# Overflow tiles of a mixture of experts: up products in high and low halves, weights loaded in two parts

## The reference, cut to what matters

```python
scores = softmax(t @ gate_w.T)
weights, indices = top_k(scores, 2)
y = zeros_like(t)
for e in range(16):
    w_e = sum(where(indices == e, weights, 0.0), axis=-1)
    y = y + ((silu(t @ w1[e].T) * (t @ w3[e].T)) @ w2[e].T) * w_e[:, None]
z = (silu(t @ sw1.T) * (t @ sw3.T)) @ sw2.T
x = x + tanh(g_ffn[1]) * (y + z)
```

## Time and profile before

| | us |
|---|---|
| median of three executions | 909.65 |
| the profiled execution | 908.75 |
| its span, first to last instruction | 907.0 |
| first up product of an overflow tile starts | 840.63 |
| down product of the last tile starts | 883.00 |
| granted TensorE clock, mean over the span | 0.997 of full speed |

### The profile page before, as it was taken

The page is one execution under the profiler, slowest core; times in us unless marked ns, Lnnn a source line. Parts: engine busy times, 40 slices in busy tenths (PEclk is TensorE's granted clock), DMA queues, the critical chain, the costliest instruction groups (busy, mean ns, idle before and its releaser), DMA issues.

```text
span 907.0 us, 16248 instructions
## 1 busy us (share of the span) xinstructions
PE 885.2 (98%) x6896; PEld 726.0 (80%) x6896; DVE 506.5 (56%) x787; ACT 349.2 (39%) x510; POOL 153.2 (17%) x146
## 2 busy tenths in 40 slices
PE   5999999999999999999999999999999999999997
PEld 5968787878787878788999888887788888877656
DVE  5554454453545455785344344699657387776225
ACT  4633424334333333665253311344652454444110
POOL 0022223132223131210000000014003312222110
PEclk9999999999999999999999999999999999999999
DMA  9011010101020103049900100700221599999837
GB/s 342 20 36 36 1 35 1 35 1 36 1 83 1 36 1 116 1 95 275 303 14 1 44 4 0 285 1 2 109 84 67 206 348 362 358 359 313 294 138 267
DMA packets 30760, 106.87 MB, mean 118 GB/s; under 512 B 3522, under 2 KB 4546, under 8 KB 26978
## 3 DMA queue, kind: packets, MB, share of 16 engines
q1 hardware_dynamic: 25154, 87.46, 27.9%
q0 software_dynamic: 4672, 16.82, 5.8%
q10 hardware_dynamic: 864, 1.57, 0.5%
HBM read 87.18 MB, written 18.66 MB: 117 GB/s over the span
## 4 chain that ended last, share of the span: by engine, by line
PE 87%; DVE 7%; ACT 3%; issue 1%; POOL 0%; DMA 0%; DVEq 0%; ACTq 0%; POOLq 0%
PE ps L645 21%; PE ps L646 19%; PE ps L647 19%; PE ps L1116 6%; PE ps L707 3%; PE ps L1102 3%; PE ps L722 2%; PE ps L923 2%; PE ps L921 2%; PE ps L922 2%; PE ps L755 1%; PE ps L1064 1%; PE ps L1065 1%; PE ps L1066 1%; DVE arena L1828 1%
## 5 line engine op out<-in xcount | busy, mean ns | idle before, releaser
L645 PE MATMUL ps<-arena_r 128*125 128x512 f32 (+2 forms) x544 | 206.8, 380 | 2.9 <-DVE arena_r L1533 2.9
L646 PE MATMUL ps<-arena_r 128*125 128x512 f32 (+2 forms) x544 | 198.9, 366 | 0.0
L647 PE MATMUL ps<-arena_r 128*125 128x512 f32 (+2 forms) x544 | 198.8, 366 | 0.0
L645 PE MATMUL ps<-hT,arena_r 128*128 128x448 f32 (+1 forms) x368 | 136.5, 371 | 0.5 <-DVE hT L1563 0.3
L647 PE MATMUL ps<-hT,arena_r 128*128 128x448 f32 (+1 forms) x368 | 134.5, 366 | 0.0
L646 PE MATMUL ps<-hT,arena_r 128*128 128x448 f32 (+1 forms) x368 | 134.5, 365 | 0.0
L645 PEld LDWEIGHTS ps<-arena_r 128*125 128x125 f32 (+1 forms) x544 | 102.7, 189 | 21.9 <-issue 4.0
L647 PEld LDWEIGHTS ps<-arena_r 128*125 128x125 f32 (+1 forms) x544 | 102.3, 188 | 13.9
L646 PEld LDWEIGHTS ps<-arena_r 128*125 128x125 f32 (+1 forms) x544 | 102.6, 189 | 10.9
L1190 ACT ACTIVATE arena<-arena,mbias,mscale 125x448 f32<-125x448 f32 x96 | 66.1, 752 | 99.5 <-DVE arena L1640 99.5
L2093 POOL TENSOR_TENSOR arena<-arena 125x448 f32<-125x448 f32 x28 | 32.3, 1154 | 259.0 <-ACT arena L1190 259.0
(11 more groups left out here) (252 smaller groups left out, 1328.5 us busy)
## 6 DMA issues: line engine op xcount, KB each, us to landing
land_e<-in_e SPq DMA_DIRECT2D x16, 1408.0 KB, 7.9
arena<-in_e SPq DMA_DIRECT2D x21, 512.0 KB, 7.6
sorted_rows<-arena POOLq DMA_DIRECT2D x1, 7453.0 KB, 60.6
arena<-in_e SPq DMA_DIRECT2D x5, 1408.0 KB, 6.4
land_c<-in_ctx SPq DMA_DIRECT2D x8, 752.0 KB, 4.4
arena<-sorted_rows SPq DMA_DIRECT2D x21, 257.0 KB, 10.1
land_w<-in_gu SPq DMA_DIRECT2D x8, 512.0 KB, 17.9
arena<-in_e SPq DMA_DIRECT2D x21, 192.0 KB, 9.8
```

The costliest lines, as they stand in the source:

```text
L645: mm(into, a[0], w[0], start=begins and i == 0, stop=False)
L646: mm(into, a[0], w[1], start=False, stop=False)
L647: last = mm(into, a[1], w[0], start=False, stop=ends and i == len(operands) - 1)
```

## The change

The up products of the overflow tiles are formed from high and low parts, as those of tiles 0 to 15 are. ACT's `rows_save` is replaced by `rows_high`, and ACT gets `overflow_high`, two copies of 128x1408 per tile. DVE gets `overflow_low`, two subtractions of 128x1408 per tile, and `rows_low`. The order of weights and rows on SP's queue changes: the up weights come as two transfers of 128x1408, half 0 counted on `up_ld[0]` together with the rows, half 1 on `up_ld[1]`; the down weights stay on `dn_ld[0]`. `w_landed` goes up by three per tile instead of two. The wait for half 0 and the rows of the tile before stands at the head of SP's turn, and the next half 0 is issued behind it, before the wait for half 1.

```diff
-            def load_up_of(e, n):
-                sp.dma_start(arena[:, bass.ds(A_E + n % NSLOT * 4352, 2816)],
-                             e13_in[bass.ds(e, 1)].rearrange("o p w -> p (o w)")).then_inc(up_ld[0], 16)
+            def load_up_of(e, n, half):
+                sp.dma_start(land_x[:, bass.ds(n % NSLOT * 4352 + half * 1408, 1408)],
+                             e13_in[bass.ds(e, 1), :, half * 1408:(half + 1) * 1408].rearrange("o p w -> p (o w)")
+                             ).then_inc(up_ld[half], 16)
...
             with sp.Fori(NE + 1, tiles) as n:
                 e = expert_of(n)
+                sp.wait_ge(up_ld[0], n * 32)
+                sp.sem_inc(w_landed, 1)
                 sp.wait_ge(gu_mm, n - 3)
                 sp.wait_ge(row_read, n - 3)
-                load_up_of(e, n)
+                load_up_of(e, n, 0)
+                load_rows_of(n)
+                sp.wait_ge(up_ld[1], n * 16)
+                sp.sem_inc(w_landed, 1)
+                load_up_of(e, n, 1)
                 sp.wait_ge(dn_ld[0], n * 32)
                 sp.sem_inc(w_landed, 1)
                 sp.wait_ge(d_mm, n - 3)
                 load_down_of(e, n)
-                sp.wait_ge(up_ld[0], n * 32 + 32)
-                sp.sem_inc(w_landed, 1)
...
             def up_expert(n):
-                w = A_E + n % NSLOT * 4352
-                pe.wait_ge(w_landed, n * 2 + 1)
-                pe.wait_ge(xg_sv, n + 1)
+                pe.wait_ge(w_low, n * 2 + (nth("sh2") + 2))
+                pe.wait_ge(ln_T, n + (4 * NT + 1))
+                high, low = n % 2 * (28144 - A_E13), A_E - A_E13 + n % NSLOT * 4352
                 for j in range(2):
-                    for k in range(KC):
-                        last = mm(ps[:, 4 + j, 0:EI], xgT[:, k, :],
-                                  arena[:, bass.ds(w + (k * 2 * EI + j * EI), EI)], start=k == 0, stop=k == KC - 1)
+                    last = product(ps[:, 4 + j, 0:EI], [([half[:, k, :] for half in xgT_r],
+                                                         [split_x[:, bass.ds(half + (k * 2 * EI + j * EI), EI)]
+                                                          for half in (high, low)]) for k in range(KC)])
                 last.then_inc(gu_mm, 1)
...
+            def overflow_high(n):
+
+                high, low = n % 2 * (28144 - A_E13), n % NSLOT * 4352
+                for i in range(2):
+                    act.wait_ge(w_landed, n * 3 + (i + 1))
+                    fn(split_x[:, bass.ds(high + i * 1408, 1408)], land_x[:, bass.ds(low + i * 1408, 1408)], ACT.Copy
+                       ).then_inc(w_high, 1)
...
             with act.Fori(NE - 1, last2) as n:
                 silu_tile(n)
-                rows_save(n + 1)
+                rows_high(n + 1)
                 place(n + 2)
+                overflow_high(n + 2)
...
+            def overflow_low(n):
+
+                high, low = n % 2 * (28144 - A_E13), n % NSLOT * 4352
+                for i in range(2):
+                    dve.wait_ge(w_high, n * 2 + (nth("sh2") + i + 1))
+                    v.tensor_tensor(split_x[:, bass.ds(A_E - A_E13 + low + i * 1408, 1408)],
+                                    land_x[:, bass.ds(low + i * 1408, 1408)],
+                                    split_x[:, bass.ds(high + i * 1408, 1408)].bitcast(F32), ALU.subtract
+                                    ).then_inc(w_low, 1)
...
             with dve.Fori(NE + 1, last1) as n:
+                overflow_low(n + 1)
                 tile_hidden(n)
+                rows_low(n + 1)
                 row_ends(n + 1)
                 tile_out(n - 1)
                 tile_hidden_save(n)
```

More of the change, by code:

```diff
@@ L242, in flamingo @@
         land_e = [landing(f"land_e{i}", A_W[i], 2816) for i in range(NSLOT)]
+        land_x = landing("land_x", A_E, (NSLOT - 1) * 4352 + 2816)[1]
         e13 = [halves((4352, 28144)[e % 2], A_W[e % NSLOT], land_e[e % NSLOT], KC, 2 * EI) for e in range(NE)]
@@ L250, in flamingo @@
         smoe = at(10184, EI)
-        xgT = at(47616, KC, P)
-        xgT_r = at_r(47616, KC, P), at_r(31000, KC, P)
+        xgT_r = [nc.alloc_sbuf_tensor_at(name, [P, KC, P], F32R, offset=base + 4 * off)[:]
+                 for name, off in (("xg_high", 47616), ("xg_low", 31000))]
+        A_E13 = 4352
+        split_x = nc.alloc_sbuf_tensor_at("split_x", [P, 28144 + 2816 - A_E13], F32R, offset=base + 4 * A_E13)
         A_XR = 44288
@@ L593, in _ @@
             sp.wait_ge(up_ld[0], 16 * NE)
-            load_up_of(e, NE)
+            load_rows_of(NE)
+            load_up_of(e, NE, 0)
+            sp.wait_ge(up_ld[1], 16 * NE)
+            load_up_of(e, NE, 1)
             sp.wait_ge(d_mm, NE - 4)
@@ L615, in _ @@
                 load_down_of(e, n)
-                sp.wait_ge(up_ld[0], n * 32 + 32)
-                sp.sem_inc(w_landed, 1)
+            sp.wait_ge(up_ld[0], tiles * 32)
+            sp.sem_inc(w_landed, 1)
+            sp.wait_ge(up_ld[1], tiles * 16)
+            sp.sem_inc(w_landed, 1)
             sp.wait_ge(dn_ld[0], tiles * 32)
@@ L1111, in down_expert @@
                 else:
-                    pe.wait_ge(w_landed, n * 2 + 2)
+                    pe.wait_ge(w_landed, n * 3 + 3)
                 if not (isinstance(n, int) and n == 0):
@@ L1459, in _ @@
             last3, last2, last1, tiles = counts(act)
-            def rows_save(n):
-                act.wait_ge(xg_tr, n + 1)
-                fn(xgT, ps[:, 6, :].rearrange("p (k t) -> p k t", k=KC), ACT.Copy).then_inc(xg_sv, 1)
             def silu_tile(n):
@@ L1469, in place @@
             def place(n):
-                act.wait_ge(w_landed, n * 2 + 1)
+                act.wait_ge(w_landed, n * 3 + 1)
                 if not (isinstance(n, int) and n == NE):
@@ L1492, in _ @@
                     expert_high(n + 2)
+            def overflow_high(n):
[4 more added lines that the diff above has]
+                       ).then_inc(w_high, 1)
             act.sem_inc(xs_rdy, NE)
             place(NE)
+            overflow_high(NE)
             with act.Fori(NE - 1, last2) as n:
                 silu_tile(n)
-                rows_save(n + 1)
+                rows_high(n + 1)
                 place(n + 2)
+                overflow_high(n + 2)
             silu_tile(last2)
-            rows_save(last1)
+            rows_high(last1)
             silu_tile(last1)
@@ L2042, in _ @@
                     expert_low(n + 2)
+                else:
+                    overflow_low(n + 2)
             tile_hidden(NE)
+            rows_low(NE + 1)
             row_ends(NE + 1)
```

5 lines of the change are left out of this document (2 added, 3 removed).

## The result

| | before | after |
|---|---|---|
| median, us | 909.48 (20 executions) | 912.34 (20 executions) |
| lowest and highest, us | 907.13, 911.94 | 906.77, 916.12 |
| ratio of the times | | 1.0031, 95% interval 1.0021 to 1.0041 |
| profiled execution, its span | 908.75, 907.0 | 910.41, 908.5 |
| first up product of an overflow tile starts | 840.63 | 839.66 |

The changed kernel is slower by about 0.3%, 2.8 us. That is less than the 0.5% called telling ahead of the prediction, but with twenty executions of each the interval excludes no change. The forecast was 0.3 us less than before.

A forecast was written before the change was run, and what follows sets the result against it. PE, 87% of the chain, was taken as nearly level with the chain of output scatters. Waits ate most of PE's -4.1 us; mostly the early -0.8, plus 0.5 for scatters, gave -0.3 us: 909.3 us, range 906.0 to 912.9.

The forecast's parts named there:

- PE's product: Up products of the five overflow tiles: 3.92 us instead of 4.74 each, -4.1 us on PE if nothing delays it.
- Addresses on PE: Address instructions in the up blocks of tiles 17 to 20: +2.9 us if fully exposed, taken as hidden, 0.
- Rival C: PE's sequencer: addresses are exposed in the overflow up products, +1 to +2.6 us, 911.5; chance 0.06.
- the last up load issued before 858: Sign on SP's queue: tile 20's up load, which went out at 860.23 before, is issued earlier than 858.
- is worth nothing to PE directly: SP's last load ending 3 to 4 us earlier gains PE nothing directly, since no row has PE waiting for a load.
- add half a microsecond for scatters 13 to 15: Output scatters of tiles 13 to 15 share the DMA engines with denser loads: +0.5 us.
- DVE as the pacemaker behind the gap: After tile 16's output copy, tile 19's up product waits for DVE's subtractions and `rows_low`, until 866.6 instead of 865.17.
- "early" case: Loads end earlier, so tile 17's output copy comes at 867.1, not 869.33; tile 20's up product ends 0.8 us earlier.
- Rival A: Scatters of tiles 13 to 15 land in some 5 us each, tile 16's copy never late: -1.5 to -4.7 us; chance 0.15.
- Rival D: Half 1 of tile 20's up weights lands late, so ACT, DVE and `rows_low` end late: +0.9 us; chance 0.05.
- Rival B: DVE's subtractions hold POOL's scatter issue for tile 16, +3.8 us, or tile 17 too, +5.4, 915.0; chance 0.08.
- own range of the forecast: Overflow tiles: -0.8 us to +2.3, the upper end with three scatters at 6.7 us each and tile 17's copy late.

The follow-up runs named there:

- old_loads_again: Second run of the changed kernel with SP's queue as in the kernel before (whole up loads, late wait): 909.37 us, 0.9985 of before.
- one_early: Changed kernel with up weights in one transfer, its wait at the head of SP's turn: 912.93 us, 1.0030 of before.
- late_split: Changed kernel with both waits for the up halves moved to the end of SP's turn: 911.99 us, 1.0030 of before.
- after_again: The changed kernel measured once more, nothing altered: 911.81 us, 1.0022 of before.
- new_loads: Kernel before with plain products and only SP's queue of the change (halves, early waits): 914.72 us, 1.0049 of before.
- halves_late: Kernel before with plain products, up loads in halves, both waits at the end of SP's turn: 910.28 us, 1.0011 of before.

## Why the prediction was off

- **PE's product, -4.1 us: right.** 3.92 to 3.97 us against 4.74, five times. The 3.56 us that the prediction set beside it didn't show, as rows 3 had said.
- **Addresses on PE, 0: right.** L660's address instructions take 46 ns at the median, 125 at most, and the block with them is 0.05 us longer than the one without. Rival C has no part. The trace's answers on two single lines of the changed kernel, L660 and the scatters of L2207 (durations in ns, min/median/max; then from issue to landing):

```profile
L660 PEldq FUSED_REGOPS  x32: 46/46/125, 847.5 to 877.6; - x32
...
L2207 POOL DMA_INDIRECT token_rows<-arena,to_row x5: 976/977/2371, 864.7 to 889.7; - x5
...
DMA to landing us min/median/max: 2.7/4.0/6.1
```


- **SP, "the last up load issued before 858": right**, 853.75 and 856.07. That it "is worth nothing to PE directly" holds for the early loads; the halves are another matter. With whole loads PE waits up to 1.06 us at a time behind the split weights (`old_loads_again`; 1.29 in `one_early`), with late halves 0.37 (`late_split`), which the prediction didn't see. What it does to the scatters is where the sum failed.
- **The step that failed: "add half a microsecond for scatters 13 to 15, which now share the DMA engines with denser loads".** The copy of tile 16 came 3.55 us later, seven times as much, in two parts. The three scatters took 863.18 - 842.81 = 20.37 us, 6.8 each, against 860.60 - 842.15 = 18.45 before: +1.9, about the upper bound that I had worked out (1.7, from 6.7 each) and not the half microsecond that I took. And the first of them went out 842.81 - 839.66 = 3.15 us after the up product of tile 16 began, against 842.15 - 840.63 = 1.52: +1.6, which no term of mine held, because I let the delay begin only at that scatter; the one ahead of it, of tile 12, took 9.0 us against 7.1. The split is that of one execution. In `after_again` the three scatters took 21.35 us, +2.9, and the first of them went out 1.61 us after the up product, as before. Over all runs only the first part holds (20.4 to 22.9 us against 17.8 to 19.3). I took the denser loads for a small correction to a scatter that the trace had shown under light load, and the early end of the loads for the main thing.
- **A term that was missing: the clock.** After 5.29 us without work the down product ran at a granted clock of 0.56 and took 2.05 us longer. The sum priced idle time at its own length.
- **DVE as the pacemaker behind the gap: covered up.** The sum let the up product of tile 19 wait for the subtractions. It didn't: the slow down product ran until 869.47, and `rows_low`, which had begun at 867.82 and took 0.68, was done by then. Where the gap is short the wait is there: in `old_loads_again` PE waits 0.37 us for the hidden product and 0.19 for `xg_low` in that turn.
- **The "early" case, -0.8: its mechanism was right.** Behind the loads' end the scatters of tiles 16 and 17 were out of the way: the copy of tile 17 was released by PE, 1.14 us after DVE was free, and the turn of tile 19 took 7.20 us against 8.73. With the cheaper product of tile 20 that gave back 2.4 us (1.53 and 0.84 above). It came behind a gap that was larger than what it could give. The engines were nearly empty there in part because of that gap: the loads were over when the late scatter of tile 16 went out (share 0.15).
- **Rival A** (scatters out of the way) described the second half only. **Rival D** isn't in the trace.
- **Rival B** (DVE holds POOL up) is half right. The issues at 864.69 and 871.28 took 2.03 and 2.37 us instead of 0.98, since they began within a subtraction that had started at 864.25 and 871.17. Both end 0.85 to 0.86 us after that subtraction's end (864.25 + 1.62 = 865.87, and the issue ends at 866.72). So the issue is held for one subtraction, not for both. Here it cost nothing, as the copies that follow were released by PE. In `late_split` it does: it is 1.05 of the 9.07 us there. The inference in the Trainium skill, "SBUF — State Buffer", section "Who interferes with whom", that descriptor generation isn't held by such an instruction, does not agree with these rows, and the measurement decides.
- **What would show it wrong.** "PE idle for about 2 us before the down product of tile 17" was 5.29. "The output copy of tile 16 released by a scatter at 860 to 862" was 863.18. The sign "a scatter takes over 9 us" could tell nothing, as one had taken 9.7 before. The predicted range, 906.0 to 912.9, holds 912.34, near its upper end, but that is no merit of the sum: the own range of the forecast, -0.8 to +2.3, ended just short of +2.8.

**What stays open.** Why the scatters take longer as loads go out early is seen only as the DMA engines' share (840 to 862: 1.01 at 346 GB/s after, 0.86 at 289 before), and in the missing quick scatter; which part of a transfer waits wasn't measured. Two early half loads with a scatter issued first were not tried, nor two output buffers for all overflow tiles. Why late halves cost 0.3% with the products in high and low parts and late whole loads nothing isn't settled: the two differ by one profiled scatter and their intervals overlap.

## What to carry to other kernels

A load that nobody waits for is not free to move: ask which transfer on the same DMA engines somebody does wait for. Here up loads that went out 2 to 5 us earlier saved PE next to no wait and lengthened three chained scatters by 2 to 3 us. With the early loads, two output buffers instead of one at the first overflow tile brought 1.0031 down to 0.9971; the cheaper products alone, with the old loads, gave nothing that could be measured (1.0003 and 0.9985). And price a gap on TensorE at more than its length: what follows may run at the lower clock.

## What the runs showed of the hardware

- After gaps of 3.38 (`new_loads`), 5.29 (after), 5.58 (`one_early`) and 5.60 us (`after_again`) TensorE's next product ran at a granted clock of 0.54 to 0.65 and took 4.2 to 4.9 us, where it took 2.68 in the kernel before. After the gap of 2.40 us in `late_split` it stayed at 1.00; after the one of 2.04 that followed there, it didn't (0.64).
- An indirect DMA that GpSimd begins to issue while DVE subtracts two operands of 128x1408 in SBUF ends 0.8 to 0.9 us after that subtraction, and so takes up to 2.4 us and not 0.98 (2.03 in most cases, 1.19 in `old_loads_again` at 852.87, which began late in the subtraction). While the overflow tiles run, it is so at least once in each kernel that splits their weights, and never in `new_loads` and `halves_late`, which don't.
- A scatter of 128 rows landed in 2.7 us where no load runs, took up to 9.7 in the kernel before and 9.07 in `late_split`, where its issue was held and loads ran. The same scatter took 3.59 us when it went out 1.13 us ahead of a load of 128x2816 (`old_loads_again`), and 8.13 when it went out 0.38 us ahead (`one_early`).
